# Attention and mixture-of-experts layer: work of the last batches placed behind the first max transpose

## What is computed

```
xn  = layernorm(x)
q, k, v = xn @ Wq.T, xn @ Wk.T, xn @ Wv.T        # 16 heads of 8
q, k = rope(q), rope(k)                          # angle depends on the batch only: a scale per channel
att = softmax(q k^T / sqrt(8)) v                 # per batch and head, 512 x 512 scores
topk_idx, topk_w = router(xn, gate_w, e_bias)    # sigmoid, 4 of 8 groups, 6 of 32 experts
moe = sum over experts of combine * (relu(xn @ up.T)^2 @ down.T)     # 32 experts of width 64
shared = relu(xn @ shared_up.T)^2 @ shared_down.T                    # width 256
out = x + att + moe + shared
```

## Time and profile before

| | us |
|---|---|
| median of 3 runs | 695.84 |
| lowest and highest | 695.26, 709.89 |
| the profiled execution | 697.23 |
| its span in the profile | 695.4 |

### The profile page before, as it was taken

How to read it: one execution, slowest core, us unless ns; L and a number is a source line. 1 busy time by engine, 2 the same in 40 slices (tenths; PEclk the granted TensorE clock), 3 DMA queues, 4 the chain that set the end, 5 groups by cost and what they waited for, 6 DMA issues and landing times. The chain is left out here.

```text
span 695.4 us, 11331 instructions
## 1 busy us (share of the span) xinstructions
PE 672.9 (97%) x3902; PEld 343.3 (49%) x3902; DVE 486.5 (70%) x1114; ACT 401.5 (58%) x771; POOL 411.7 (59%) x344
## 2 busy tenths in 40 slices
PE   6897999999999999999999999999999999999996
PEld 5342355445554454555555454555544555445443
DVE  6585668678776878678776968678766968676500
ACT  2453356665566555665656656665656656665662
POOL 5691246665675557565676557564766556566555
PEclk9896599999999999999999999999999999999999
DMA  7838032543463343533463343542463343332210
GB/s 202 257 73 243 6 92 65 184 95 90 123 193 87 91 109 96 186 95 71 123 213 81 77 118 103 188 99 57 115 213 96 72 114 92 95 93 64 72 22 15
DMA packets 53224, 77.84 MB, mean 112 GB/s; under 512 B 5296, under 2 KB 19504, under 8 KB 53040
## 3 DMA queue, kind: packets, MB, share of 16 engines
q1 hardware_dynamic: 51440, 75.56, 40.9%
q10 hardware_dynamic: 1728, 1.57, 0.9%
HBM read 57.19 MB, written 19.40 MB: 110 GB/s over the span
## 5 line engine op out<-in xcount | busy, mean ns | idle before, releaser
L628 DVE TENSOR_REDUCE nmax<-sc 128x1 f32<-128x512 f32 x512 | 330.8, 686 | 157.0 <-PE sc L792 155.0
L453 ACT ACTIVATE probs<-st 128x512 f32<-128x512 f32 x512 | 278.9, 595 | 243.2 <-PE st L802 234.8
L338 POOL TENSOR_TENSOR gated<-gate_at,relu 128x512 f32<-128x512 f32 x128 | 162.9, 1273 | 245.0 <-ACT relu L458 244.8
L792 PE MATMUL sc<-stacks 33*128 33x512 f32 x512 | 204.0, 469 | 6.3 <-DVE nmax L628 3.3
L802 PE MATMUL st<-stacks 35*128 35x512 f32 x512 | 191.2, 454 | 1.7 <-DMA stacks<-m_parts 1.7
L802 PEld LDWEIGHTS st<-stacks 35*128 35x128 f32 x512 | 78.6, 187 | 208.8 <-issue 104.4
L342 POOL TENSOR_TENSOR g<-gated,relu 128x512 f32<-128x512 f32 x128 | 163.2, 1275 | 18.6 <-PE acc L819 0.5
L819 PE MATMUL acc<-dn,g 128*128 128x128 f32 x1024 | 139.3, 279 | 1.4 <-POOL g L342 1.4
L813 PE MATMUL pv<-probs,v_aug 128*32 128x512 f32 x1024 | 138.1, 612 | 0.0
L819 PEld LDWEIGHTS acc<-dn,g 128*128 128x128 f32 x1024 | 126.5, 193 | 16.7 <-issue 13.5
L837 PE MATMUL upb<-xnT,up 128*128 128x512 f32 x256 | 133.5, 604 | 0.0
(11 more groups left out here) (102 smaller groups left out, 397.2 us busy)
## 6 DMA issues: line engine op xcount, KB each, us to landing
gate_at<-gate_rows SPq DMA_DIRECT2D x64, 512.0 KB, 6.7
q_stack<-qk_parts SPq DMA_DIRECT2D x32, 256.0 KB, 6.5
stacks<-q_stack SPq DMA_DIRECT2D x64, 128.0 KB, 2.5
stacks<-k_stack SPq DMA_DIRECT2D x64, 128.0 KB, 2.7
k_stack<-qk_parts SPq DMA_DIRECT2D x28, 256.0 KB, 5.7
gate_at<-in_x SPq DMA_DIRECT2D x8, 256.0 KB, 5.0
x_res<-in_x SPq DMA_DIRECT2D x8, 256.0 KB, 3.2
out<-y SPq DMA_DIRECT2D x8, 256.0 KB, 2.2
```

The source lines that it names most:

```text
L338: nc.gpsimd.tensor_tensor(gated[:, u % 2, :], gate_at[:, group % RING, u % GATES, :], relu[:, u % RELUS, :], ALU.mult).then_inc(gated_read ...
L453: nc.scalar.activation(probs[:, u % 2, h, :], st_b[h % 2][:], ACT.Exp).then_inc(probs_ready, 1)
L628: nc.vector.tensor_reduce(out=nmax[:, s % 2, at:at + 1], in_=sc_b[i % 2][:], op=ALU.max, axis=AXX, negate=True).then_inc(s_read, 1)
L792: nc.tensor.matmul(sc_b[i % 2][:], stacks[rows, s % NQ, 0, pr, qt * P:(qt + 1) * P], stacks[rows, s % NQ, 1, pr, :], start=True, stop=True ...
```

## The change

PRELUDE has 36 instead of 20 warm transposes ahead of the transpose of batch 1, and q and k of batch 3 behind those of batch 2, ahead of std(2), the first sigmoid and the scores. BESIDE keeps the work of batches up to 5 (12 items instead of 22), in another order. What it loses, the transposes and projections of batches 6 and 7 and the logits of batches 4 to 7, stands in a new list BEHIND; TensorE does one item of it after each of the eight scores that follow the first max transpose, and ScalarE does its part after `load_max(0)`. The gate transpose waits for `xnT` of six batches, the transpose of batch 6 for the copy of the maxima, since both use the bank `tr`. SP waits for the landing of the first max rows before it issues the stores of batch 1 and all that follows them.

```diff
-        PRELUDE = [("warm", 32), ("x", 0), ("warm", 6), ("q", 0), ("k", 0), ("logits", 0), ("warm", 20), ("x", 1),
-                   ("warm", 6), ("q", 1), ("k", 1), ("x", 2), ("x", 3), ("q", 2), ("k", 2), ("std", 2), ("sig", 0)]
-        BESIDE = [("q", 3), ("k", 3), ("logits", 1), ("x", 4), ("logits_out", 1), ("q", 4), ("k", 4), ("x", 5),
-                  ("v", 0), ("q", 5), ("k", 5), ("shared", 0), ("x", 6), ("shared", 1), ("q", 6), ("k", 6),
-                  ("x", 7), ("gate", 0), ("q", 7), ("k", 7), ("logits", 2), ("logits_out", 2)]
+        PRELUDE = [("warm", 32), ("x", 0), ("warm", 6), ("q", 0), ("k", 0), ("logits", 0), ("warm", 36), ("x", 1),
+                   ("warm", 6), ("q", 1), ("k", 1), ("x", 2), ("x", 3), ("q", 2), ("k", 2), ("q", 3), ("k", 3),
+                   ("std", 2), ("sig", 0)]
+        BESIDE = [("logits", 1), ("x", 4), ("v", 0), ("logits_out", 1), ("q", 4), ("k", 4), ("shared", 0),
+                  ("x", 5), ("shared", 1), ("q", 5), ("k", 5), ("gate", 0)]
+
+        BEHIND = [("x", 6), ("q", 6), ("k", 6), ("x", 7), ("logits", 2), ("q", 7), ("k", 7), ("logits_out", 2)]
...
             load_gates(0)
+            sp.wait_ge(m_ld[0], MAXES * 16)
             store_parts(1)
...
-            for kind, i in PRELUDE + BESIDE:
+            for kind, i in PRELUDE + BESIDE + [("max", 0)] + BEHIND:
...
+                elif kind == "max":
+                    load_max(0)
...
-            load_max(0)
...
+                if i == 6:
+                    pe.wait_ge(m_ready, 1)
...
                 elif kind == "gate":
-                    pe.wait_ge(xnT_ready, B)
+                    pe.wait_ge(xnT_ready, 6)
                     gate_transpose(0)
...
             max_transpose(0)
             for i in range(FIRST_AHEAD):
                 score(TILES + i)
+                for kind, n in BEHIND[i * len(BEHIND) // FIRST_AHEAD:(i + 1) * len(BEHIND) // FIRST_AHEAD]:
+                    prelude(kind, n)
```

## The result

| | median us | lowest, highest | executions |
|---|---|---|---|
| kernel before | 697.80 | 695.26, 709.89 | 5 |
| changed kernel | 715.36 | 714.28, 718.32 | 5 |

What follows compares the result with a forecast made beforehand. TensorE was taken to bind, by only 3.4 us over VectorE in the sixteen scores. -1.3 - 0.7 + 5.2 - 1.5 = +1.7 us gave 698.9 profiled, median 697.5; range 688 to 704.

Steps and rivals of the forecast that it cites:

- The slow clock: First scores: TensorE's clock falls at about 31 instead of 27.9 and returns at about 38, a spell as long as before.
- Rival (c): From 31 the clock stays at 1.2 GHz until the maxima; unit 4 at 104.6, +12 us, time 707.8; chance 0.08.
- The second fall: Sixteen scores, near 47 to 49: TensorE idle about 2.3 us; if the clock falls, max transpose at 57.05, not 54.05.
- Rival (b): The clock falls near 47 and again in unit 0; unit 4 at 97.6, +4.9 us, time 700.8; chance 0.25.
- Start of the scores: Before and during first scores: std(2) late at 26.9, TensorE waits 1.5 and 1.7 us, score 3's maximum 1.3 us earlier.
- The sixteen scores: First score to max transpose: 6.9 us of TensorE work leaves, VectorE becomes the bound, max transpose at 54.05, 2.0 us gained.
- Behind the max transpose: Max transpose to unit 0: moved work makes the stretch 12.7 us where 7.5 stood, a term of +5.2 us.
- Units 0 to 3: The clock falls in unit 0 and stays low for units 1 and 2: 27.6 us instead of 29.10, -1.5.
- The other bound: Units 0 to 3 all at full clock would take 21.1 us.
- rival (a): The clock holds in the units, 21.1 us; unit 4 at 87.85, -4.8 us, time 691.0; chance 0.30.
- The hold: SP's stores of batch 1 wait for the max rows, which land under TensorE's work: 0 us, at most 1.7.
- The warm transposes: Ahead of the transpose of batch 1: 16 more take 1.9 us, hidden behind late xn, costing 0 to 0.1 us.

Runs made afterwards that it cites:

- e12: Changed kernel with idle transposes at every TensorE wait, 3 behind each head of unit 0 and 18 ahead of unit 1's second max transpose: 697.28 us, ratio 1.0004.
- e5: Changed kernel with idle transposes wherever TensorE waited in the run with two filled waits, 4 behind each head of unit 0: 703.16 us, ratio 1.0064.
- e6: Kernel before with 36 warm transposes and idle ones behind k2, the eight scores (2 each, 14 behind the last) and unit 0's heads: 704.66 us, ratio 1.0072.
- e13: Kernel before, order untouched, with 36 warm transposes and idle ones at its waits, 1 behind each of the eight scores, 18 in unit 1: 693.11 us, ratio 0.9960.
- e2: Changed kernel with 17 idle transposes ahead of logits 1 and 13 ahead of the transpose of batch 4: 711.14 us, ratio 1.0162.
- e4: Kernel before with only q and k of batch 3 put ahead of std(2) and the scores: 711.26 us, ratio 1.0148.
- e8: Kernel before with 36 instead of 20 warm transposes and nothing else: median 705.95 us, ratio 1.0011.
- e11: Kernel before with 36 warm transposes; last logits, their transpose and q and k of batch 7 moved behind the max transpose: 704.28 us, ratio 1.0066.
- e15: Changed kernel with 32 idle transposes in one piece behind the transpose of logits 1: 718.49 us, ratio 1.0300.
- e9: Kernel before with only the eight items of batches 6, 7 and the last logits moved behind the max transpose: 710.12 us, ratio 1.0159.

## Why the prediction was wrong, step by step

**The slow clock, the step that failed.** The prediction gave the spell that begins at 31 the length of the one before ("a spell as long as before", to 38), and priced the case in which it lasts at +12 us with a chance of 0.08, arguing "with the same work it came back at 34.5". It lasted to 112. The work was not the same: the new slots have one item between scores where the old ones had logits 1 and x4 together at 31.1 to 34. A group (37.5) and a burst (40.5) brought the clock back, one item at a time did not for 82 us in the changed kernel, yet did so at 33.3 in the run with q and k of batch 3 back. What brings it back is therefore not settled. Rival (c) was the one that named what happened: the max transpose at 60 (60.5 measured), unit 0 at 77 (81.0), unit 4 at 104.6 (113.8). Its chance was too small and its price of 12 too low.

**The second fall.** Rival (b) named it in the right stretch: the grouped and the filled run, the one with q3 back and the one with the move alone all fell at 44 to 47, in or just behind waits of 1.3 to 1.9 us for VectorE (2.3 foreseen). Only the last two fell beside the last piece of routing, as it said; the first two fell 2 to 3 us earlier, beside pieces whose TENSOR_SCALAR took 1.48 and 1.87 us. The prediction took VectorE's pieces at the length of one trace, and these lengths change from run to run. The sentence of the Trainium skill that the prediction set against this change (TensorE: Matmul & The Clock Gate, section "A second HAM failure mode: psum-queue depth-cycling": repeated short idle stretches make the clock go back and forth) agrees with these four traces as far as they fall behind short waits, one to three times each; in the changed kernel the clock did not go back and forth, but fell once and stayed down. I took 54.05 because no row of before showed such a fall; the row of an idle 1.92 us and a fall behind it was near enough to give it more weight. It would not have made it certain: TensorE was idle for 1.88 us ahead of 17.70 in the same trace, and no fall followed.

**Start of the scores.** Right as to order, late in time: std(2) at 27.88 (26.9 said), GpSimd's batches 4 to 7 from 29.44 (28.5), waits of 2.13 and 0.68 us on TensorE (1.5 and 1.7); 1.0 of it is that this execution reached its first score 1.0 later. The second wait is shorter as the logits ran at the slow clock into it. The maximum of score 3 came at 34.55 (33.5 plus 1.0 said): right.

**The sixteen scores.** The gain of 2.0 became a loss of 3.4. The -1.3 of it, "score 3 comes earlier", came true (its maximum stands 7.37 us behind the first score, 8.67 before), but behind it "VectorE becomes the bound" failed: TensorE at half rate was the bound, with 28.79 us busy of 33.32, VectorE 21.20. No filled run shows the gain either: 26.84 and 27.4 us (e12, e5) from the first score to the max transpose in the changed order, 26.8 in both filled runs of the old one (e6, e13). The -1.3 is gone there, since it was a gain over scores at 1.2 GHz: that maximum stands 6.47 us behind the first score in e12 and 5.56 in e13. But neither run is clean, as e12 has 3.4 us at 1.2 GHz in this stretch and in e5 the CAST behind the last maximum took 2.26 us (0.17 in e13), so a gain of 1 us or so at full clock is not excluded.

**Behind the max transpose.** +5.2 said, at full clock: 13.41 - 8.48 = 4.9 measured in the filled pair, and 5.9 against the 7.48 of the kernel before. The 8.48 have the spell of 3.4 us in them and 12 fills at the slow clock (2.82 us), so 4.9 is rather the lower bound. The mechanism was right, the number in part luck: the terms of the prediction, 1.5 + 1.3 + 4.8 + 0.4 + 5.4 + 0.8, make 14.2 and not its 12.7, and the 13.41 lie between. With 14.2 the forecast would have been 699.0. At the slow clock the estimate of 17 in (c) was too low: 20.4 to 20.7 in all runs that were slow there (20.45 in the changed kernel). Of its 13.0 us over the kernel before, then, some 6 (13.41 - 7.48) are order and some 7 (20.45 - 13.41) clock. It is the largest term of the loss.

**Units 0 to 3.** 27.6 said, 32.87 measured; the runs whose clock came back in unit 2 as before (e2: 29.1) support the form of the estimate, but here it came back only in unit 3, during the value projection and the expert slice (109.8 to 113), which cost 3.8 more. The other bound, 21.1 at full clock, was too low: 24.0 in both filled runs (with their fills, which stood where TensorE waited). So rival (a), warm units, is worth 5 us, not 8.

**Edits costed at nothing.** The hold: 0 said, 715.36 with it and 715.48 without, as said. The warm transposes: 0 to 0.1 said, ratio 1.0011 with an interval of 0.55% each way; but half of the executions are outside the ratio, and the medians of all differ by 5.8 us, so this term is not shown.

The sum in these terms, for the profiled execution: +1.0 (start), +3.4, +13.0 and +3.8, some 21 us; order accounts for about 5 to 6 of them, the long spell for the rest. The medians say the same: filling gives back 18.1 us in the changed kernel (715.36 to 697.28) and 3.7 in the kernel before (696.84 to 693.11). That the slow clock is the loss is shown by this; why it stayed low for 82 us in this order is open.

## What to carry to other kernels

Where a stretch runs close to the bound of two engines, taking work from TensorE does not only uncover the other engine's time: it opens waits in which TensorE's clock can fall, and what stands behind them runs slower until it is back (here a pair of products 2.07 us instead of 1.02). Before moving work, look at what TensorE does in each microsecond beside the other engine's longest piece, give a fall there a price and a real chance, and give a price too to the case in which the clock does not come back soon. Take the length of the other engine's pieces from more than one execution. To tell order from clock, fill the waits with idle transposes in both versions and compare those; and fill only real waits, since a fill that is not covered is work.

## What the runs showed of the hardware

TensorE stayed at 1.2 GHz for 82 us in the changed kernel, although it was busy for 24.78 of 26 us in a part of it. In several traces it came back behind stretches of full-row products or transposes without the 33-row scores (31.1 to 34.0 before, a group to 37.5, 32 transposes to 40.5, value projection and expert slice to 112.3). In others scores stood in between: at 33.3 in the run with q and k of batch 3 back, and at 105.4 in the one without the hold.

It often fell in or behind waits of 1.0 to 2.9 us. But it fell also where no such wait stood: in the kernel before at 58.4, where no wait was above 0.8 us and thin scores stood alone; in e13 at 58.4, in a stretch where TensorE was busy 8.48 of 8.48 us with thin scores and single fills; in e12 at 41.3, behind a wait of 0.66. And it did not fall behind the idle 1.88 us ahead of 17.70 in the kernel before. So these runs do not tell from a wait alone whether the clock will fall. Where in a trace it falls varies from execution to execution of one and the same kernel: the slow clock of the kernel before was 29 to 65 us in its executions, and the time 695 to 713 with it, about 0.5 us for each us.

VectorE's small instructions do not have one length beside GpSimd. The TENSOR_SCALAR of 128x4 in the last piece of routing took 1.19 us before, 0.93 in e13, and 2.80 or 2.81 in e4, e8, e11 and e15; the CAST of 128x16 behind the last maximum took 0.17 before, 2.26 in e5 and 2.62 in e9. Four of them read beside GpSimd's timeline end within 0.03 us of the end of a GpSimd instruction: 48.57 and 48.54 before, 53.09 and 53.07 in e8, 54.81 and 54.79 in e5, 54.49 and 54.47 in e9. That GpSimd holds them up is the likely reading, but no run varied it. Several of the waits of TensorE in which the clock fell stand beside such an instruction (1.94 in e2, 2.67 in e8, 2.77 in e4).

The costs do not add. Each part of the change alone cost 12.5 to 13.1 us (e9, e4), the whole 17.6. And with one wait filled the clock fell at the next (30.4, then 44.9, then 57 and 80.9), while each further fill paid a part: 715.4, 711.1, 703.2, 697.3.
